# A two-layer convolution kernel: the kernels of its last stage expanded in plain float32 on four row groups of TensorE

## The reference, cut to what matters

```python
r = relu((x @ Wr + br - mean) * rsqrt(var + eps) * gamma + beta)   # 64 -> 16 numbers a pixel
w = r @ Ws + bs                     # 16 -> 16 groups x 9 taps
xi = x @ Wi + bi                    # 64 -> 64
out = sum over the taps of w[group(channel), tap] * shifted xi
x = x + out
```

## Time and profile before

| | |
|---|---|
| time, median of 3 runs | 686.87 us (686.27 to 687.97) |
| time of the profiled execution | 687.15 us |
| its span, first to last instruction | 685.4 us |
| mean granted clock of TensorE | 0.988 of full speed |
| last stage (first expansion to the end) | from 463.5 us of the span on |
| busy over the span: PE, DVE, ACT, POOL | 95%, 80%, 42%, 25% |

### The profile page before, as it was taken

The page is one execution under the profiler, slowest core; times in us unless marked ns, Lnnn a source line. Parts: engine busy times, 40 slices in busy tenths (PEclk is TensorE's granted clock), DMA queues, the critical chain, the costliest instruction groups (busy, mean ns, idle before and its releaser), DMA issues.

```text
span 685.4 us, 14823 instructions
## 1 busy us (share of the span) xinstructions
PE 649.0 (95%) x6176; PEld 265.6 (39%) x6176; DVE 551.1 (80%) x901; ACT 287.1 (42%) x370; POOL 172.6 (25%) x156
## 2 busy tenths in 40 slices
PE   6867999999999999999999989999999999999995
PEld 7533333333333333333333333333444444444542
DVE  5699866989988988995577787848888888888885
ACT  3754622323231422143102400043677777677661
POOL 2100420009102700450041110411344234234230
PEclk9999999999999999999999999999999999999998
DMA  9920000000000000000000000000011121121122
GB/s 327 214 56 1 2 1 1 1 1 2 2 1 1 2 1 1 1 2 1 1 13 4 1 1 2 1 1 1 20 44 33 42 52 33 34 60 33 32 62 63
DMA packets 54511, 19.67 MB, mean 29 GB/s; under 512 B 51154, under 2 KB 51892, under 8 KB 54452
## 3 DMA queue, kind: packets, MB, share of 16 engines
q1 hardware_dynamic: 54164, 18.57, 11.2%
q10 hardware_dynamic: 288, 0.21, 0.1%
HBM read 10.39 MB, written 8.39 MB: 27 GB/s over the span
## 4 chain that ended last, share of the span: by engine, by line
PE 72%; DVE 17%; ACT 1%; issue 1%; DVEq 0%; ACTq 0%
PE conv L670 36%; PE att L740 11%; PE conv L724 10%; PE att L460 4%; PE att L539 4%; DVE comb L1264 4%; DVE xpad L1183 3%; PE att L712 2%; PE att L551 2%; PE conv L636 2%; DVE x L1484 2%; DVE stats L1278 2%; PE att L518 1%; DVE x L1241 1%; DVE x L1240 1%
## 5 line engine op out<-in xcount | busy, mean ns | idle before, releaser
L670 PE MATMUL conv<-xpad,comb 64*64 64x512 f32 x2592 | 289.0, 593 | 4.8 <-DVE x L1248 2.9
L1484 DVE TENSOR_TENSOR x<-conv,x 128x512 f32<-128x512 f32 x288 | 179.0, 683 | 26.6 <-PE conv L724 25.3
L670 PEld LDWEIGHTS conv<-xpad,comb 64*64 64x64 f32 x2592 | 96.6, 133 | 173.7 <-issue 160.0
L1264 DVE SCALAR_TENSOR_TENSOR comb<-experts,wsel,comb 128x576 f32<-128x576 f32 (+1 forms) x138 | 112.8, 885 | 9.5 <-ACT comb L852 9.4
L724 PE MATMUL conv<-rstack,wse 98*128 98x512 f32 x288 | 96.3, 445 | 1.9 <-DVE xin L1273 0.9
L852 ACT ACTIVATE comb<-experts,wsel 128x576 f32<-128x576 f32 (+2 forms) x52 | 37.2, 768 | 112.7 <-PE conv L670 71.7
L740 PE MATMUL att<-x,cmp 64*32 64x512 f32 x1280 | 79.7, 596 | 0.0
L724 PEld LDWEIGHTS conv<-rstack,wse 98*128 98x128 f32 x288 | 49.5, 189 | 60.9 <-DVE x L1484 46.6
L1183 DVE SCALAR_TENSOR_TENSOR xpad<-att,x 128x1024 f32<-128x1024 f32 x46 | 53.9, 1214 | 19.8 <-PE att L518 19.6
L1621 POOL TENSOR_TENSOR x<-x,xin 128x1024 f32<-128x1024 f32 x15 | 35.9, 2396 | 115.2 <-ACT x L992 115.2
L862 ACT ACTIVATE x<-conv,bias 128x512 f32<-128x512 f32 x40 | 25.2, 681 | 83.5 <-PE conv L670 83.4
(11 more groups left out here) (186 smaller groups left out, 610.8 us busy)
## 6 DMA issues: line engine op xcount, KB each, us to landing
x<-in_x SPq DMA_DIRECT2D x32, 256.0 KB, 5.2
out<-comb SPq DMA_DIRECT2D x30, 256.0 KB, 3.2
experts<-in_We SPq DMA_DIRECT2D x1, 1152.0 KB
out<-comb SPq DMA_DIRECT2D x4, 128.0 KB, 2.2
wide<-in_c_wide SPq DMA_DIRECT2D x1, 192.0 KB, 5.6
x<-in_c_sum SPq DMA_DIRECT2D x1, 160.0 KB
small<-in_c_small ACTq DMA_DIRECT2D x1, 142.5 KB, 4.0
map_sel<-in_c_map SPq DMA_DIRECT2D x1, 128.0 KB
```

Of the source, the lines that this page charges most:

```text
L670: last = nc.tensor.matmul(conv[own[to], h, HW * rows:HW * rows + HW], comb[own[rows], q % 2, n, tap(t)], xpad[own[rows], 2 * (q % 2) + n, ...
L1264: v.scalar_tensor_tensor(comb[:, q % 2, n, cols], experts[:, e, cols], wsel[:, p % 2, j + QP * n, e:e + 1], comb[:, q % 2, n, cols], ALU.m ...
L1484: v.tensor_tensor(img(prod[i])[:, rows, :], img(conv[:, unit, :])[:, rows, :], xip[s][:, kh + 16 * h:kh + 16 * h + 16, kw:kw + W], ALU.mul ...
```

## The change

- `wse` is one plain float32 copy of the weights for 17 rows (16 of `Ws` and one of `bs`) x 64 columns per tap, held four times, at partitions 0, 32, 64 and 96. The split into high and low parts, `masks` and their work on ACT, POOL and DVE are gone.
- `wr` is 32 columns wide (16 of `Wr`, 16 of zeros). `project` makes 8 matmuls of 64 rows x 32 columns x 512: row group g (32 partitions) gets half `g % 2` of the pixels of both images, side by side in two banks; groups 2 and 3 are copies of 0 and 1.
- `empty_r` is one ACT operation, 128 x 1024, straight into `rstack`. The row of ones comes from the relu (scale 0, bias 1 in the parameters). The second ACT copy and POOL's `r_lo` are gone.
- `expand` makes per tap and half two float32 matmuls, one per image: 17 rows x 64 columns x 512. Half h of a tap uses row group `h + 2 * unit`, so that two consecutive taps use all four row groups and both column halves. The waits on DVE and the order on PE are as before.
- `LATE_CONSTS` is 9 DMAs instead of 8; the loads of `masks` and four of the six of `Wr` are gone.

```diff
-        wse = sb("wse", [RR, TAPS, 128], F32R)
+        wse = sb("wse", [128, TAPS, C])
...
-        rstack = sb("rstack", [128, 2, S], F32R)
+        rstack = sb("rstack", [128, 2, 2, HW])
...
-        wr = sb("wr", [128, AR])
+        wr = sb("wr", [128, RG])
...
-        BLOCKS += [(wr[64 * n:64 * n + 64, 32 * a + CR * n:32 * a + CR * n + CR], A["Wr"])
-                   for n in range(2) for a in range(PARTS)]
+        BLOCKS += [(wr[64 * n:64 * n + 64, 0:CR], A["Wr"]) for n in range(2)]
...
-            def project(k, s, m, weights, rows):
+            def project(k, s, m):
...
-                for h, cols in halves():
-                    last = nc.tensor.matmul(att[0:rows, 1, cols], weights, xn[s][:, cols], start=True, stop=True)
+                for copy in range(2):
+                    for n in range(2):
+                        for h, cols in halves():
+                            g = h + 2 * copy
+                            last = nc.tensor.matmul(att[RG * g:RG * g + RG, 1, HW * n:HW * n + HW], wr[own[n], :],
+                                                    xn[s][own[n], cols], start=True, stop=True)
...
                 if i == 0:
-                    eng.wait_ge(rstk_ready, k + 1)
+                    eng.wait_ge(misc_free, 1 if isinstance(k, int) and k == 0 else 3 * k)
                 for h, cols in halves():
                     if not (isinstance(k, int) and k == 0 and i < 2):
                         eng.wait_ge(prod_ready, 2 * (e - 2) + h + 1)
-                    nc.tensor.matmul(conv[:, unit, cols], wse[:, ORDER[i], :], rstk[s][0:RR, cols],
-                                     start=True, stop=True).then_inc(exp_full, 1)
+                    first = RG * (h + 2 * unit)
+                    for n in range(2):
+                        last = nc.tensor.matmul(conv[own[n], unit, cols], wse[first:first + RR, ORDER[i], :],
+                                                rstk[s][first:first + RR, n, :], start=True, stop=True)
+                    last.then_inc(exp_full, 1)
...
-            def empty_r(k, s, m):
+            def empty_r(s, m):
                 eng.wait_ge(misc_full, m + 1)
-                if not (isinstance(k, int) and k == 0):
-                    eng.wait_ge(rstk_ready, k)
-                nc.scalar.activation(r96, att[0:AR, 1, :], ACT.Relu, bias=rsc[:, 3:4], scale=rsc[:, 1:2])\
-                    .then_inc(misc_free, 1)
-                eng.wait_ge(misc_free, m + 1)
-                nc.scalar.activation(rstk[s][0:AR, :], r96, ACT.Copy).then_inc(rhi_ready, 1)
+                nc.scalar.activation(rstk[s], att[:, 1, :].rearrange("p (n c) -> p n c", n=2), ACT.Relu, bias=rsc[:, 3:4],
+                                     scale=rsc[:, 1:2]).then_inc(misc_free, 1)
...
-                v.tensor_tensor(rstk[s][32:64, :], r96[32:64, :], rstk[s][32:64, :].bitcast(F32), ALU.subtract)\
-                    .then_inc(rstk_ready, 1)
```

More of the change, by code:

```diff
@@ L37 @@
 PARTS = 3
-AR = 96
-RR = 98
+RG = 32
+RR = 17
 T = S // 128
@@ L201, in build @@
         st_sum = stage[:, 0:(TAPS + 1) * 32]
-        st_ws = stage[0:RR, 1152:1152 + TAPS * G16]
-        st_exp = stage[0:RR, 1296:1296 + TAPS * C]
-        st_bd = stage[0:RR, 1872:1872 + TAPS * 128].rearrange("p (t c) -> p t c", t=TAPS)
+        st_ws = stage[:, 1152:1152 + TAPS * G16]
         conv = ctx.enter_context(nc.psum_tensor("conv", [128, 2, S], F32))
@@ L294, in build @@
         pix = [pixels[:, n, :].rearrange("p (t c) -> p t c", t=T) for n in range(2)]
-        rstk = [rstack[:, n, :] for n in range(2)]
+        rstk = [rstack[:, n, :, :] for n in range(2)]
         def sum_of(n, h):
@@ L601, in beside @@
                         eng.wait_ge(att_free[1], sum(u == 1 for u, _ in ATT_USES))
-                        project(0, 0, 0, wr[:, :], AR)
+                        project(0, 0, 0)
                     elif at == (3, 1, 2):
@@ L755, in involve @@
                 if not last:
-                    project(k + 1, 1 - s, m, wr[:, :], AR)
+                    project(k + 1, 1 - s, m)
                 expand(k, s, 4)
@@ L894, in expanded_weights @@
                 late.then(nc.scalar.activation(
[L895 to L900, removed]
+                    wse[:, :, :].rearrange("p t c -> p (t c)").rearrange("p (g j t) -> p g j t", g=G16, j=C // G16),
+                    st_ws.rearrange("p (g t) -> p g t", g=G16).unsqueeze(2).to_broadcast([128, G16, C // G16, TAPS]), ACT.Copy))
                 late.then(nc.scalar.activation(sum_sel[:, :, :].rearrange("p a b -> p (a b)"), st_sum, ACT.Copy))
@@ L1426, in _ @@
                         group_norm(att[:, use.unit, 0:2 * GP], slice(0, GP), GP, (att_full[use.unit], use.full), (att_free[use.unit], use.freed))
-                        eng.wait_ge(late_lo, 2)
-                        hi_of = wse[:, :, :].rearrange("p a b -> p (a b)")
-                        v.scalar_tensor_tensor(hi_of, hi_of.bitcast(F32), masks[:, 3:4], st_bd.rearrange("p t c -> p (t c)"),
-                                               ALU.mult, ALU.add).then_inc(wse_ready, 1)
                     if q - 1 >= QP * LAST:
@@ L1596, in _ @@
                 route_beside(p)
-            eng.wait_ge(late_setup, LATE_STEPS - 1)
-            bd = st_bd.rearrange("p t c -> p (t c)")
-            v.tensor_tensor(bd, bd, wse[:, :, :].rearrange("p a b -> p (a b)").bitcast(F32), ALU.subtract).then_inc(late_lo, 1)
-            eng.wait_ge(late_lo, 1)
-            v.tensor_scalar(bd, bd, masks[:, 2:3], None, ALU.mult).then_inc(late_lo, 1)
             modulated(eng, QUADS - 1)
@@ L1622, in finish @@
                 eng.wait_ge(fin_ready, k + 1)
-            def involve(k, s, first=False, last=False):
-                if not first:
-                    finish(k - 1)
-                if not last:
-                    r_lo(k + 1, 1 - s)
-            eng.wait_ge(late_lo, 2)
-            r_lo(0, 0)
-            involve(0, 0, first=True)
             inverse_root(5, slice(GP, NP), GP)
-            with eng.Fori(0, GP - 1) as i:
-                involve(2 * i + 1, 1)
-                involve(2 * i + 2, 0)
-            involve(NP - 1, 1, last=True)
+            with eng.Fori(0, NP - 1) as k:
+                finish(k)
 def constants():
@@ L1652, in constants @@
             total[:, c, t + upper if t == TAPS // 2 else t + (t > TAPS // 2), o] = 1
-    row = np.arange(RR)
-    low = ((row >= 64) & (row < 96)) | (row == 97)
-    masks = np.stack([(row % 32 < CR) | (row >= AR), (row % 32 >= CR) | (row >= AR), low, ~low], 1).astype(np.float32)
     return {
@@ L1683, in small_constants @@
         pick.reshape(128, -1), both(a["L0_conv_be"].T), all_rows(np.tril(np.ones((K, K)), -1)),
-        np.tile(rpar, (128 // CR, 1)), below, all_rows(a["L0_conv_alpha"]), both(a["L1_conv_bi"].reshape(C, 1)),
+        np.tile(np.concatenate([rpar, np.tile([0, 0, 1, 0, 1], (CR, 1))]), (4, 1)), below, all_rows(a["L0_conv_alpha"]), both(a["L1_conv_bi"].reshape(C, 1)),
     ], 1).astype(np.float32))
```

36 lines of the change are left out of this document (10 added, 26 removed).

## The result

The changed kernel takes 719.57 us (median of 4, 718.99 to 724.84), the kernel before in the same comparison 686.84: 1.049 times as long, interval 1.044 to 1.054. Slower, as forecast, and 7.6 us above the forecast of 712.0.

The account below looks back on a forecast made before the run. PE was taken to set the end, DVE 1.7 us a pair behind. 687.15 us plus 24.8 (15 periods), plus 1.0 (first pair), minus 0.9 (first projection) gave 712.0 us; own range 698 to 723, whole range 698 to 738.

Parts of the forecast that it names:

- a walk over one pair: One middle pair written out between PE and DVE: period 14.67 us against 13.02, 1.95 of it PE's waits.
- rival 1: Expansion passes of 17 rows by 64 columns are quicker than 0.43 us, so waits cost little: 682 us, chance 0.10.
- The removed work: POOL's subtraction, second ACT copy, `wse` preparation and saved DMAs were hidden already; their going gains zero.
- Rival 2: Expansion halves issued at different times don't overlap on PE, 35 us more: 747 us, chance 0.07.
- the signs that I named: Profile signs: right if period 14.3 to 14.9 us and DVE pieces break PE's chain; wrong if last-stage clock below 1.
- The total: 15 periods from the first pair's end to the last's, each 14.67 instead of 13.02 us: 24.8 us more.
- 1.06 us: Time from an expansion's start on PE to its bank being full for DVE; bounds 0.97 and 1.18.
- Transposes 0.80: PE's transposes in each pair, taken as 0.80 us without the change of mode.
- the second of the two waits: In the block of taps 0 and 1, PE's last half waits 0.41 us for tap 8's products.
- First pair: 1.0 us in all: First pair's products are paced by DVE up to tap 5; tap 8 comes 1.0 us later by slower expansion.
- the last pair ... 0.2 us more, which I leave out: Last pair, without projections in both kernels: its difference is 0.2 us more than a middle pair's, not counted.
- rival 3: Granted clock falls to half in a stretch of each pair, 1.7 us each, 25 in all: 737 us, chance 0.06.

Follow-up runs that it names:

- the run without the split: Kernel before, without the second ACT copy and POOL's subtraction, relu writing straight into `rstack` (expanded kernels not right): 686.98 us, ratio 1.001.
- the ends filled: Changed kernel plus five projections whose results nobody reads, three in the first pair and two in the last: 716.22 us, ratio 1.044 to the kernel before.
- the other order of blocks: Changed kernel with PE's order expand 4; add_up 0; expand 5, 6; project_xi; add_up 1; expand 7, 8; add_up 2: 714.78 us, ratio 1.040.
- the one-pass one: Changed kernel with `wse` and `rstack` in bfloat16, one instruction per expansion matmul instead of two, lower precision: 674.45 us, ratio 0.983 to the kernel before.
- PE filled: Changed kernel with bfloat16 `wse` and `rstack`, projection doubled in every pair and extra unread projections in the first and last pair: 670.67 us, ratio 0.976.
- the two-part kernel: Changed kernel redone with stacked high and low bfloat16 parts, 50 rows by 64 columns, 64-row groups, one pass per expansion: 668.34 us, ratio 0.974.

## Why the prediction was right, and where it was off

**The direction and the mechanism** stood. The forecast was a walk over one pair, and the trace of the changed kernel follows it nearly piece by piece:

- Sizes: the 16 passes of a block on 8 tiles take 0.86 (taps 6 and 7: 1.04 with the change). The edit that was hardest to bound, a pass of 17 rows by 64 columns, costs 0.43 as the wider ones do: rival 1 fell, with its 682 us.
- The block of taps 4 and 5: 2.22 measured, 2.28 forecast (2.12 and the change). Taps 6 and 7: 1.04, forecast 1.02. Projection, add_up, project_xi, expand 8: to the hundredth. DVE's gaps: 3.62, forecast 3.56, the largest 1.61 both times, in front of tap 6. PE's waits: 1.99, forecast 1.95.
- The changes between 32x64 and 64x32, taken as 0.16 from another pair of small tiles: measured 1.88 - 1.72 and 1.02 - 0.86, 0.16, and 0.18 in front of taps 6 and 7.
- The removed work was worth nothing (the run without the split: 1.001).
- Rival 2 fell: the block of taps 4 and 5 takes 2.22 us, where halves without overlap need 3.44.
- Of the signs that I named, one of the right ones did not come: PE's chain isn't broken by DVE pieces, it shows PE alone. And one of the wrong ones came: a granted clock below 1 in windows of the last stage.

**What was mis-sized.** The forecast was +24.9, the profiled spans say +32.8; 7.9 us are missing.

- "The total": 15 x (14.67 - 13.02). The period is 14.81, and 15 x 0.15 = 2.2 us. In the walk four stretches make up the period: add_up 3 and 4, 1.88; from the start of taps 2 and 3 to the end of taps 4 and 5, which goes through one full bank and four products, 4.60; from add_up 0 to add_up 2, 4.78; from the start of tap 8 to the end of taps 0 and 1, through one full bank and two products, 3.41. Measured they are 1.88, 4.66, 4.80 and 3.47. The term that was too small is the time to a full bank, "1.06 us", which is 1.12 and counts twice a pair.
- "Transposes 0.80" had no row behind it: the earlier trace rows have 0.89 without any change of mode, and 1.09 was measured, 0.13 more than 0.80 + 0.16. It cost nothing. It lies inside the second of the two waits, so the block of taps 0 and 1 waits that much less (1.36 for the walk's 1.27 + 0.16, although its bank is full 0.06 later). Taps 2 and 3 are in the same way 0.13 longer than in the walk without moving the end of taps 4 and 5 by more than the 0.06.
- "First pair: 1.0 us in all", "the last pair ... 0.2 us more, which I leave out" and rival 3: the other 5.7 us. They sit in the first pair, 1.8 (of which the earlier start of this execution hides 0.5), in the second, 1.2, and in the last, 3.2 beyond the longer period. I gave the granted clock a chance of 0.06 and one price, in each pair or in none. It happened in the first two pairs and the last only; in the first and the last, work of a neighbouring pair is missing between the blocks. The rows for it were there: the kernel before already falls to half clock in its first pair, and the changed kernel makes just these pieces narrower and slower. The step that failed is the walk over the ends: it used the middle's clock, and the last pair's walk, with neither projection to fill the block of taps 4 and 5, should have been priced at the clock of such a stretch. An estimate from these rows: 6.8 us at half clock cost the last pair at most 3.4, which leaves 17.3 - 3.4 = 13.9 us at full clock, 1.6 more than before; the walk had 1.65 + 0.2 there. So the walk was sound at full clock, and the clock was the part that it lacked.

That the time still lies within the forecast's own range, 698 to 723, is in part luck: its upper end was made of dearer changes of tiling and later banks, and nearly three quarters of the missing 7.9 us came from something else.

With the ends filled, the first and the last pair give back 1.71 + 2.33 = 4.0 us in the profiled executions, 3.4 in the medians. The rest of the 5.7 is mostly the second pair's stretch at half clock. What brings that one about stays open: it is there with the first pair filled (480.8 to 484.2), and it isn't there with the other order of blocks, whose first pair has the longer one. I have no run that changes one thing between the two.

## What to carry to other kernels

When two engines pass a few buffers to and fro, don't compare sums of work; write one period out by hand, with the time from the start of an instruction to its result in the right column. Here the sum for PE fell from 13.0 to 12.8 us and the period rose to 14.8, because a bank was full 1.12 instead of 0.54 us after its start and the last half of a block took 0.86 instead of 0.23. Walk the first and the last period on their own, and take the granted clock of the nearest such stretch for them, not the middle's.

## What the runs showed of the hardware that I had not expected

- **Extra work on PE can shorten a kernel.** Repeated projections that nobody reads took 3.4 us off the changed kernel and 3.8 off the one-pass one; the granted clock of the profiled executions went from 0.971 to 0.990 and from 0.967 to 0.987. The Trainium skill (TensorE: Matmul & The Clock Gate, A second HAM failure mode: psum-queue depth-cycling) describes a clock that swings when PE idles shortly between groups of matmuls; the one-pass kernel's windows (0.57 at 543 to 547 us, 1.00 with PE filled) agree. How much idle time brings a fall isn't shown here, and the busy time in a window doesn't tell: the two-part kernel has PE idle for 1.9 of 40 us (500 to 540) and keeps its clock through the middle, the one-pass kernel with 2.2 of 40 doesn't, and with the ends filled the clock falls at 480.8 behind 8.00 busy us of 8.00.
- **And it can be worth nothing:** in the two-part kernel, where DVE is the busiest engine, filling removed PE's half clock in the first pair and the time stayed (668.34 and 668.49 us).
- **Tiles of separate row groups overlap even if they are released one by one.** Halves issued as their banks came free still shared the array with the ones before them; without the second pair of row groups each pair of taps took 1.88 us, wherever it stood.
- **The change of tile mode costs about the same, 0.16 to 0.18 us,** between 32x64 and 64x32 as between 64x64 and 64x32 (0.16), and 0.20 from 32x64 to the whole array of the transposes (1.09, with 0.89 in the kernel before).
